# A convolution block and a two-way selective scan on one core: layer norm in a stage of its own, or slice by slice beside the scan

## The reference, cut to what matters

```python
h = gelu(_bn(einsum(conv17x17(_bn(x)), pw_weight)))
x = residual + gamma * h * a[:, :, None, None]
# second block: tokens = the 4096 pixels
xn = (xh - mu) * lax.rsqrt(var + 1e-05) * ln_g + ln_b     # over the 96 channels
def _mamba(x_seq):
    x, z = split(x_seq @ W_in)                             # 192 channels each
    x = silu(causal_conv4(x, conv_w, conv_b))
    proj = x @ W_xproj
    dt = softplus(proj[..., :6] @ W_dt + b_dt)
    Bm, Cm = proj[..., 6:22], proj[..., 22:]
    y = selective_scan(x, dt, Bm, Cm, -exp(A_log), D)      # h = exp(dt A) h + dt B x;  y = h C + x D
    return y * silu(z) @ W_out
out = _mamba(x_seq) + flip(_mamba(flip(x_seq)))
```

## Time and profile before

| | |
|---|---|
| median of the runs | 5559.85 us (5557.4, 5559.85, 5569.05) |
| the profiled execution, own time | 5567.16 us |
| its span | 5565.3 us |
| mean granted TensorE clock | 0.818 |
| `normalise` | 461.7 to 612.9 us |
| `scan` | first scan at 684.3, last ends 5501.6 us |

### The profile page before, as it was taken

The page is one execution under the profiler, slowest core; times in us unless marked ns, Lnnn a source line. Parts: engine busy times, 40 slices in busy tenths (PEclk is TensorE's granted clock), DMA queues, the critical chain, the costliest instruction groups (busy, mean ns, idle before and its releaser), DMA issues. The chain is left out here.

```text
span 5565.3 us, 77050 instructions
## 1 busy us (share of the span) xinstructions
PE 4537.5 (82%) x18064; PEld 1235.1 (22%) x18064; DVE 5198.8 (93%) x3757; ACT 3300.4 (59%) x5416; POOL 4820.8 (87%) x2295
## 2 busy tenths in 40 slices
PE   5878578878888888888888888888888888888887
PEld 4553111111222112122111212211122211112222
DVE  5556489999999999999999999999999999999998
ACT  1237556656666666666666666666666666666665
POOL 0020189999999999999999999999999999999998
PEclk9999777777888888888888888888888888888887
DMA  2237555565666666666666666666666666666666
GB/s 75 75 94 235 171 168 183 186 199 191 210 195 195 200 208 208 200 206 198 195 201 209 204 202 203 198 196 201 213 198 208 197 200 198 202 214 195 211 196 203
DMA packets 365956, 1062.76 MB, mean 191 GB/s; under 512 B 71396, under 2 KB 119926, under 8 KB 315340
## 3 DMA queue, kind: packets, MB, share of 16 engines
q1 hardware_dynamic: 355724, 1045.89, 58.2%
q10 hardware_dynamic: 8064, 14.16, 0.8%
q0 software_dynamic: 1984, 1.06, 0.1%
HBM read 849.20 MB, written 211.63 MB: 191 GB/s over the span
## 5 line engine op out<-in xcount | busy, mean ns | idle before, releaser
L1476 POOL TENSOR_TENSOR hc<-hring,c_rep 128x1024 f32<-128x1024 f32 x1541 | 3604.2, 2364 | 82.0 <-DVE hring L1431 78.8
L1431 DVE TENSOR_TENSOR_SCAN hring<-decay,carry,u_ps 128x1024 f32<-128x1024 f32 x1157 | 2670.3, 2331 | 0.0
L1413 DVE TENSOR_TENSOR u_ps<-u_ps,u_rep 128x1024 f32<-128x1024 f32 x1157 | 1396.4, 1207 | 86.0 <-DMA u_rep<-u_scr 65.0
L1171 PE MATMUL u_ps<-stack_b,w_spread 48*128 48x512 bf16 x2314 | 856.0, 455 | 717.6 <-DVE hring L1431 713.2
L1303 ACT ACTIVATE decay<-dt_rep,w_a 128x1024 f32<-128x1024 f32 x1158 | 1325.5, 1145 | 122.4 <-DVE hring L1431 108.9
L1189 PE MATMUL y_ps<-hc,w_gather 128*32 128x512 f32 x6144 | 1036.9, 754 | 0.0
L1303 ACT ACTIVATE u_ps<-dt_rep,w_a 128x1024 f32<-128x1024 f32 x386 | 430.6, 1116 | 1008.4 <-DVE hring L1431 1004.4
L1463 POOL TENSOR_TENSOR drive_p<-u_rep,b_rep 128x1024 f32<-128x1024 f32 x386 | 912.3, 2364 | 12.1 <-DMA u_rep<-u_scr 12.1
L1431 DVE TENSOR_TENSOR_SCAN hring<-u_ps,carry,drive_p 128x1024 f32<-128x1024 f32 x385 | 900.5, 2339 | 0.0
L1171 PEld LDWEIGHTS u_ps<-stack_b,w_spread 48*128 48x128 bf16 x2314 | 134.2, 98 | 1915.2 <-DVE hring L1431 1601.8
L1212 PE MATMUL prep_ps<-xn,w_conv 128*128 128x512 f32 x792 | 459.5, 694 | 121.9 <-ACT xc L1326 95.9
(11 more groups left out here) (152 smaller groups left out, 4398.6 us busy)
## 6 DMA issues: line engine op xcount, KB each, us to landing
dt_rep<-dt_scr SPq DMA_DIRECT2D x194, 1024.0 KB, 5.9
u_rep<-u_scr SPq DMA_DIRECT2D x194, 1024.0 KB, 6.3
c_rep<-bc_scr SPq DMA_DIRECT2D x260, 512.0 KB, 4.7
b_rep<-bc_scr SPq DMA_DIRECT2D x130, 512.0 KB, 5.8
xn<-xn_scr SPq DMA_DIRECT2D x132, 384.0 KB, 5.3
y_scr<-y_sb SPq DMA_DIRECT2D x768, 64.0 KB, 1.9
xn<-xn_scr SPq DMA_DIRECT2D x132, 256.0 KB, 4.7
dt_scr<-dt_sb SPq DMA_DIRECT2D x260, 128.0 KB, 2.1
```

The source lines that it names most:

```text
L1171: mm = nc.tensor.matmul(u_ps[nv % NSLOT][:, sl], w["spread"][:, q, :], upper(stack_b[drv][:, sl]), start=True, stop=True)
L1413: nc.vector.tensor_tensor(slot[:, :], slot[:, :], u_rep[r][:, b, :], ALU.mult).then_inc(drive_ready, 1)
L1431: nc.vector.tensor_tensor_scan(hring[nv % NHR][:, ::step], factor[:, ::step], term[:, ::step], carry[:, drv, nv:nv + 1], ALU.mult, ALU.add ...
L1476: nc.gpsimd.tensor_tensor(hc[nv % NHC][:, :], hring[nv % NHR][:, :], c_rep[q][:, :], ALU.mult).then_inc(c_applied, 1)
```

## The change

Image 0 is normalised as before, by `normalise` with `over_first` in place of the loop over all images: 8 slices instead of 64. The other 56 slices are made inside `scan`, one per pass, in passes 0 to 55: pass p of chunk-iteration `it` makes a slice of the image after the one being scanned. It is done in another form, with tokens on the rows: SP loads at step 5; ACT scales the centring matrix by the image's gate at step 10; PE multiplies the slice's four blocks of 128 tokens by the gated and the plain centring matrix at steps 11 and 12 (eight matmuls, residual added by accumulation); ACT copies the result to `ntok` at step 13, squares with a sum along the row at step 14 (four), and at step 15 takes Ln and Exp of 128x4 and scales the four blocks; PE turns the blocks back at step 20, ACT applies `ln_g` and `ln_b` at step 21, SP stores at step 22. All of this on PE goes through `prep_ps` as well.

To make room in `prep_ps` the output work moves: the second `y_sum` and gating from step 10 to step 2, the projection from 12 to 10, its copy and store one step behind each, the first z product from 20 to 21. The second `y_sum` now follows `low`'s copy, the first dt matmul of step 3 waits for the second gating, and the first convolution matmul waits for `ntok`'s copy. On every engine "norm" stands right ahead of "conv", on SP behind "gate". The loops over `it` become 0 to 3 with "norm" alone, 4 to 27 with both, 28 to 31 with the output work alone. DVE gets three small memsets and nothing else. `scan` stands inside the scope of `gate` now, and the centring matrix and `ln_g`, `ln_b` are kept with the weights.

```diff
-def normalise(nc, d, gate):
+def normalise(nc, d, gate, w):
...
-                over_slices(sp, (0, load))
+                over_first(sp, (0, load))
...
-        SLICE_AT, Z_AT = 15, (20, 22)
-        SUM_Y_AT, PROJECT_AT, RES_AT, OUT_STORE_AT = (0, 10), 12, 13, 14
+        SLICE_AT, Z_AT = 15, (21, 22)
+        SUM_Y_AT, PROJECT_AT, RES_AT, OUT_STORE_AT = (0, 2), 10, 11, 12
+        NORM_IN_AT, NORM_GATE_AT, CENTRE_AT, TOKENS_AT, SQUARE_AT, SCALE_AT = 5, 10, (11, 12), 13, 14, 15
+        TURN_AT, NORM_OUT_AT, NORM_STORE_AT = 20, 21, 22
+        NORM_PASSES = 2 * (ITERS - CHUNKS)
...
             with eng.Fori(0, CHUNKS - 1) as it:
-                iteration(it, (False, False), (False, False))
-            iteration(CHUNKS - 1, (False, True), (False, False))
-            with eng.Fori(CHUNKS, ITERS) as it:
-                iteration(it, (True, True), (True, True))
+                iteration(it, (False, False), (False, False), True)
+            iteration(CHUNKS - 1, (False, True), (False, False), True)
+            with eng.Fori(CHUNKS, ITERS - CHUNKS) as it:
+                iteration(it, (True, True), (True, True), True)
+            with eng.Fori(ITERS - CHUNKS, ITERS) as it:
+                iteration(it, (True, True), (True, True), False)
...
+                        wait(sp, norm_stored, stored, not isinstance(pn, int) or pn > 1)
                         for tap, lo, hi, j, at in TAP_ROWS:
                             first = tokens(it, dr) + (tap if dr == 0 else 2 * HALO - tap)
                             sp.dma_start(xn[at:at + hi - lo, j, :], d["xn_scr"][it // CHUNKS, lo:hi, bass.ds(first, T)]).then_inc(xn_in, 16)
...
+                    if m == NORM_IN_AT:
+                        image, at = norm_slice(it, dr)
+                        free, = ready(p + 1)
+                        sp.wait_ge(centred, free)
+                        sp.dma_start(gate_now[:, :], gate_all[:, bass.ds(image, 1)]).then_inc(norm_in, 16)
+                        sp.dma_start(nh[:, :], d["act_scr"][image, :, bass.ds(at, SL)]).then_inc(norm_in, 16)
+                        sp.dma_start(nx[:, :], d["x_tok"][image, :, bass.ds(at, SL)]).then_inc(norm_in, 16)
+                    if m == NORM_STORE_AT:
+                        image, at = norm_slice(it, dr)
+                        made, = ready(p + 1)
+                        sp.wait_ge(norm_out, made)
+                        sp.dma_start(d["xn_scr"][image, :, bass.ds(at + HALO, SL)], nout[:, :]).then_inc(norm_stored, 16)
...
-                            if g == 0 and slicing:
+                            if g == 0 and beside[1]:
+                                pe.wait_ge(tokens_out, pn - 1)
+                            elif g == 0 and beside[0]:
                                 pe.wait_ge(res_ready, pn - 1 - OUT_LAG)
...
+                        if g == 0 and beside[0]:
+                            pe.wait_ge(gated, 2 * (pn - 1 - OUT_LAG) + 2)
...
-                                pe.wait_ge(prep_out, NPREP * (k + OUT_LAG + 2))
+                                pe.wait_ge(prep_out, NPREP * (k + OUT_LAG + 1) + 4)
...
+                    if m == CENTRE_AT[0]:
+                        pe.wait_ge(norm_in, 48 * (p + 1))
+                        pe.wait_ge(centrer_gated, p + 1)
+                        if slicing:
+                            pe.wait_ge(res_ready, p - OUT_LAG + 1)
+                        else:
+                            pe.wait_ge(prep_out, NPREP * (p + 2))
+                    for j in range(NBLK):
+                        if m == CENTRE_AT[j // 2]:
+                            to, tok = prep_ps[:, j * C:(j + 1) * C], slice(j * P, (j + 1) * P)
+                            nc.tensor.matmul(to, nh[:, tok], gated_centrer[:, :], start=True, stop=False)
+                            mm = nc.tensor.matmul(to, nx[:, tok], w["centrer"][:, :], start=False, stop=True)
+                            if j == NBLK - 1:
+                                mm.then_inc(centred, 1)
+                    if m == TURN_AT:
+                        pe.wait_ge(tokens_scaled, p + 1)
+                        pe.wait_ge(prep_out, NPREP * (p + 2) + 3)
+                        for j in range(NBLK):
+                            mm = nc.tensor.matmul(prep_ps[0:C, j * P:(j + 1) * P], ntok[:, j, :], w["ident"][:, :], start=True, stop=True)
+                        mm.then_inc(turned_back, 1)
...
+                    if m == NORM_GATE_AT:
+                        act.wait_ge(norm_in, 48 * (p + 1))
+                        act.wait_ge(centred, p + 1)
+                        nc.scalar.activation(gated_centrer[:, :], w["centrer"][:, :], ACT.Copy, scale=gate_now[:, 0:1]).then_inc(centrer_gated, 1)
+                    if m == TOKENS_AT:
+                        act.wait_ge(turned_back, p + 1)
+                        act.wait_ge(centred, p + 2)
+                        nc.scalar.copy(ntok[:, :, :], prep_ps[:, 0:NBLK * C].rearrange("p (j c) -> p j c", j=NBLK)).then_inc(tokens_out, 1)
+                    if m == SQUARE_AT:
+                        act.wait_ge(tokens_out, p + 1)
+                        for j in range(NBLK):
+                            mm = nc.scalar.activation(squares[:, j, :], ntok[:, j, :], ACT.Square, accum_out=nstat[:, 0, j:j + 1])
+                        mm.then_inc(norm_step, 1)
+                    if m == SCALE_AT:
+                        act.wait_ge(norm_step, 3 * p + 1)
+                        nc.scalar.activation(nstat[:, 1, :], nstat[:, 0, :], ACT.Ln, bias=neps[:, 0:1], scale=1.0 / C).then_inc(norm_step, 1)
+                        act.wait_ge(norm_step, 3 * p + 2)
+                        nc.scalar.activation(nstat[:, 2, :], nstat[:, 1, :], ACT.Exp, scale=-0.5).then_inc(norm_step, 1)
+                        act.wait_ge(norm_step, 3 * p + 3)
+                        for j in range(NBLK):
+                            mm = nc.scalar.activation(ntok[:, j, :], ntok[:, j, :], ACT.Copy, scale=nstat[:, 2, j:j + 1])
+                        mm.then_inc(tokens_scaled, 1)
+                    if m == NORM_OUT_AT:
+                        act.wait_ge(turned_back, p + 2)
+                        act.wait_ge(norm_stored, 16 * (p + 1))
+                        nc.scalar.activation(nout[:, :], prep_ps[0:C, :], ACT.Identity, bias=w["lng"][:, 1:2], scale=w["lng"][:, 0:1]).then_inc(norm_out, 1)
...
-                run(act, ("back", back), ("prep", prep), ("slice", slice_out), ("conv", conv), ("gate", gate), ("front", front))
+                run(act, ("back", back), ("prep", prep), ("slice", slice_out), ("norm", norm), ("conv", conv), ("gate", gate), ("front", front))
```

More of the change, by code:

```diff
@@ L100, in over_slices, with over_first @@
     image(B - 1, last=True)
+def over_first(eng, *stages):
+    most = max(lead for lead, _ in stages)
+    for s in range(-most, NS):
+        for lead, what in stages:
+            if 0 <= s + lead < NS:
+                what(0, s + lead)
 def over_last(eng, *stages):
@@ L1022, in front, with conv @@
                         load_u(*later(3, u, n, it, dr))
-                def conv(m, pn, it, dr, slicing):
+                def conv(m, pn, it, dr, beside):
                     if m == XN_AT:
+                        counts = (16 * (pn - 1) if beside[1] else 16 * (NORM_PASSES + 1), NPREP * (pn - 1) + 3)
+                        stored, done = ready(*counts)
                         it = it if isinstance(it, int) else it % ITERS
-                        wait(sp, prep_done, NPREP * (pn - 1) + 3, not isinstance(pn, int) or pn > 0)
+                        wait(sp, prep_done, done, not isinstance(pn, int) or pn > 0)
+                        wait(sp, norm_stored, stored, not isinstance(pn, int) or pn > 1)
                         for tap, lo, hi, j, at in TAP_ROWS:
@@ L1283, in slice_out, with norm @@
                         mm.then_inc(projected, 1)
-                run(pe, ("front", front), ("back", back), ("prep", prep), ("slice", slice_out), ("conv", conv), ("gate", gate))
+                def norm(m, p, it, dr, slicing):
+                    if m == CENTRE_AT[0]:
[3 more added lines that the diff above has]
+                            pe.wait_ge(res_ready, p - OUT_LAG + 1)
+                        else:
+                            pe.wait_ge(prep_out, NPREP * (p + 2))
[12 more added lines that the diff above has]
+                        mm.then_inc(turned_back, 1)
+                run(pe, ("front", front), ("back", back), ("prep", prep), ("slice", slice_out), ("norm", norm), ("conv", conv), ("gate", gate))
             @block.scalar
@@ L1635, in vision_mixer_kernel @@
                 pointwise(nc, d, hs, gate, w)
-            normalise(nc, d, gate)
-        scan(nc, d, w)
+            normalise(nc, d, gate, w)
+            scan(nc, d, w, gate)
     output(nc, d)
```

95 lines of the change are left out of this document (64 added, 31 removed).

## The result

| | before | changed |
|---|---|---|
| median of the runs | 5563.49 us (5557.4 to 5569.05) | 5609.96 us (5605.31 to 5612.43) |
| the profiled execution, own time | 5567.16 us | 5612.4 us |
| its span | 5565.3 us | 5610.6 us |
| first scan starts | 684.3 us | 553.0 us |
| last scan ends | 5519.5 us | 5562.6 us |

The changed kernel is slower: ratio 1.0083, 95% interval 1.0065 to 1.01, 46.5 us between the medians. The scan starts 131.3 us sooner and is over 43.1 us later, so it takes 174 us more; `output` behind it adds 2. (The time after which the table of the kernel before says that the scan's last ends, 5501.6 us, is six scans too early: its last one ends at 5519.5.)

A forecast was written before the change was run, and what follows sets the result against it. DVE was taken to bound the scan, with no engine full in `normalise`; 118 us go and 162 us come back as waits, +44, giving 5603 us. Range 5500 to 5660, the forecast's own 5580 to 5640.

The forecast's parts named there:

- What bounds: DVE full in the scan, no engine full in `normalise`; removing that stage is worth its whole length if DVE stays full.
- The term: Time removed from `normalise`: 56 slices of 2.11 us, 118 us less; the fill before the first store stays.
- Place A: Steps 2 to 6, 56 gated passes: first dt matmul held by the second gating; DVE waits 1.2 us a pass.
- Place B: Steps 15 to 17, 48 passes: ACT's scaling holds `xc`, PE's clock falls; DVE waits 2.0 us a pass.
- The sum: Whole kernel: 162 us come back in waits, 118 go, +44; 5603 us, 0.8% slower.
- The clock: PE's granted clock falls to 0.50 at both held steps, 1.2 GHz instead of 2.4, lengthening the chains before DVE's spreads.
- The covered case: Both held steps: clock stays up or delays fit DVE's slack; 0 to 0.5 us a pass, 5442 to 5470; chance 0.13.
- Place A alone: Only the wait at steps 2 to 6 appears: 5507 us; chance 0.14, shared with place B alone.
- place B alone: Only the waits at steps 15 to 17 appear: 5538 us; chance 0.14, shared with Place A alone.
- Rival 4: Low clock spreads over steps 7 to 9: 1 to 1.5 us more a pass, 5650 to 5670; 0.10 with Rival 5.
- Rival 5: SP: convolution loads wait for the previous pass's slice store and hold the queue; 5% of Rival 4.

The follow-up runs named there:

- e12: Kernel before with only image 0 normalised, in its own stage; image 0's tokens read in place of the others (result not the reference's): 5444.02 us, ratio 0.9787.
- e4: Kernel before with only the output work moved earlier (second sum and gating at step 2), normalisation still its own stage of 64 slices: 5645.02 us, ratio 1.014.
- e1: Changed kernel with the convolution's copy `xc` ahead of the norm's work in ACT's list of tasks: 5525.43 us, ratio to before 0.9929.
- e3: Changed kernel with both the edit of e1 and the edit of e2: 5449.68 us, ratio to before 0.9788.
- e2: Changed kernel with the second sum of y copied out of the shared bank by ACT, first dt matmul waiting for that copy: 5523.32 us, ratio 0.9926.
- e8: Changed kernel with three zero-weight matmuls in PE's gap at step 15, only in the 48 passes with both kinds of work: 5539.12 us.
- e9: e1 with zero-weight matmuls of 384 columns behind step 3's skip and 256 columns at step 4, in gated passes only: 5513.63 us.
- e5: Changed kernel with five zero-weight matmuls in PE's gap at step 15, in all 64 passes: 5628.56 us.
- e6: e1 with four zero-weight matmuls in PE's gaps: one at step 1, two behind step 3's skip, one at step 4: 5586.69 us.
- e7: e3 with the fills of e6 and two zero-weight matmuls in the gap at step 15, in all passes: 5591.24 us.

## Why the prediction was right

- **What bounds.** DVE full in the scan, no engine full in `normalise`, and a stage worth its whole length: e12 gives 120 to 129 us for it. The term was 118, and the changed kernel's first scan came 131.3 us sooner. It was mis-sized at both ends: the first store comes 7.0 us sooner (473.1 against 480.1), the stores take 11.1 us instead of 132.8, which is 121.7 and not 118, and the way from the last store to the first scan is 68.8 us instead of 71.4, where it was taken as unchanged.
- **Place A.** 1.2 us was said (the figures beside it, 2236.6 and 2235.3, give 1.3), 1.25 is in the trace of the pass shown, at the step said, and the times of the chain are off by 0.3 us at most. Over the 48 passes the waits there are 0.98 us on average, since 18 of them have hardly any. In time place A costs 1.37 us a pass by e4, 76.5 / 56, and 1.35 by the step from e1 to e3; the 86.6 us of e2 hold some of place B's.
- **Place B.** Six operations of ACT were put at 1.6 us and took 1.64 (2249.45 to 2251.09). The wait was put at 0.9 + 1.3 and is 0.99 + 0.86 in the pass shown, 1.76 on average; the clock came back before the second spread (0.70 us, not 1.03), and I took 2.0 for that reason. In time it is 84.5 / 48 = 1.76 us a pass by e1 and 1.53 by the step from e2 to e3.
- **The sum.** 162 us were to come back and 174 did: 48 x 3.37 + 8 x 1.5. Both halves of the account were too small, 118 by 13 us and 162 by 12, and the errors cancel, so that 5603 against 5610 is closer than the working deserved. The 3.2 us a pass, too, came out near 3.37 by luck: the waits at the two places are 0.98 + 1.76 = 2.74, and the rest is made of two things that the prediction didn't have. One is 0.16 us a pass of waits at the loop's turn, which stand neither in before nor in e4. The other is that a wait costs more than its figure: step 6 of DVE in the pass shown lasts 4.73 us where 3.37 is its length without a wait, 1.36 for a wait of 1.25. A drive and a scan in sequence overlap (2223.34 + 1.23 is past 2224.48), and a wait ends that overlap. With 3.7 waits a pass this explains most of the 0.46 us that are left.
- **The clock** was argued and is now shown: with the same hold and a higher clock the waits at B are gone (e8), and those at A in the passes where it stays up for some 3 us longer (e9, four gated passes in a row). Why it falls where it does at place A, in before as in the changed kernel, no run was made to show. Without the low clock, a hold of 2.3 us and one of 1.6 would have looked harmless beside 75 us of pass.
- **The rivals.** The covered case, 5442 to 5470 us, was at hand: e3 lies in it at 5450. Place A alone and place B alone were put at 5507 and 5538; e1, which leaves A, is 5525, and e2, which leaves B, 5523. Rival 4's third wait does exist, at step 8 in 29 of the 48 passes, but at 0.3 us each, 8.8 us in all (counted with place A above). Rival 5 has no sign: from the first scan on no wait of DVE there names a DMA. The Trainium skill ("Perfetto Trace Analysis", Optimization Strategy) holds that performance may be improved by interleaving stages that have different most-contended engines. Both outcomes are seen here: the changed kernel interleaves them and is 46.5 us slower, e3 interleaves the same work without the two holds and is 119 us faster.

## What to carry to other kernels

When work is moved beside a stage whose bound engine is full, its cost lies in the waits that it puts on the queues ahead of that engine's supplier: here the work of 56 slices cost 12 us at most and two held instructions 160. So look, for every added instruction, at what stands behind it on its queue and who waits for that, and let the read-out that frees a shared bank come first. Where an engine is only just in time, count the chain behind a hold at the clock that the trace shows there: here it stood at 0.50 behind PE's gap of 3.31 us, and the same matmuls took twice as long. And look at several passes before taking one as the rule; here 18 of 48 were of another kind.

## What the runs showed of the hardware that was not expected

- Filling PE's gap at place B moved the low clock. In e8 the granted clock from 50 to 60 us into a pass is 1.00 on average over the 48 passes, against 0.67 in the changed kernel, but from 65 to 75 us it is 0.64 against 0.89, and the mean of the run is 0.828 in both. In e5, e6, e7 and e9 the mean did rise (0.853, 0.853, 0.845, 0.843), and of these only e9 was faster than the kernel that it was built on. With the wait at the loop's turn left out, an estimate, the fill at place B is worth as much as the order of e1 (70.8 + 17 against 84.5 us), the one at place A far less than e2's copy (11.8 + 17 against 76).
- DVE's wait behind the loop's branch, with no releaser in the profile, is not there in before and e4. Where it stands it is 0.1 to 0.7 us in the kernels without fills (e12 among them) and 0.8 to 1.4 in those with fills. What sets it stays open.
- A 128x128 matmul on 512 columns of f32 took 0.9 to 1.0 us at the full clock (2.84 us for three in e8, 4.56 for five in e5), the time of two records; I had read one record as one matmul.
- The convolution stage, which no edit touches, waits for its input less in all kernels with the norm beside the scan, 129 to 133 us against 138 to 139 in before, e4 and e12 (DVE's wait of `xpad` for `xraw`), and its 6 us are in the 131.3 by which the changed kernel's scan starts sooner. What causes it stays open.
